# A graph layer on one core: VectorE's destination one-hots for the next step, made behind the row product instead of at the end of the step

## What is computed

```python
xn = layernorm(x)
# edges, self loops added; e, m, p per head
h = (xn @ W).reshape(N, 4, 64)
e = leaky_relu(a_src[src] + a_dst[dst])
p = exp(e - segment_max(e, dst)[dst])
alpha = p / segment_sum(p, dst)[dst]
gnn = relu(segment_sum(alpha[:, :, None] * h[src], dst) + bias)
# mix: q, k, v with normed k and v; kv = k^T v / N
ret = q @ kv + xn
x = x + gnn + (gelu(ret @ w1 + b1) @ w2 + b2 + xn)
# experts: top 2 of 8, two-layer network 256 -> 512 -> 256 each
xf = layernorm(layernorm(x)) * gamma + beta
x = x + sum_over_top2(weight * (gelu(xf @ W1[e] + b1[e]) @ W2[e] + b2[e]))
```

## Time and profile before

| | us |
|---|---|
| median of three runs | 2849.89 |
| lowest and highest | 2847.36 and 2851.42 |
| span of the profiled execution | 2837.7 |
| TensorE, VectorE, GpSimd, ScalarE busy | 2019.8, 1609.9, 1458.7, 1081.1 |

### The profile page before, as it was taken

One profiled execution on the slowest core, in us unless ns is written; L12 is line 12 of the kernel. 1 busy time (PEld: TensorE's weight loads), 2 busy tenths in 40 slices (PEclk: granted clock), 3 DMA queues, 4 the chain that ended last, 5 costly groups with the idle time before them and its releaser, 6 DMA issues. The chain is left out here.

```text
span 2837.7 us, 37360 instructions
## 1 busy us (share of the span) xinstructions
PE 2019.8 (71%) x9074; PEld 1433.7 (51%) x9075; DVE 1609.9 (57%) x3942; ACT 1081.1 (38%) x1932; POOL 1458.7 (51%) x1586
## 2 busy tenths in 40 slices
PE   8478887666666666666677777878777856788663
PEld 6355565445555544544445545555545544564331
DVE  7556666446575755865546656666544655553033
ACT  5222222224444533444344455555434443433110
POOL 3455555665666666553445555555553544430156
PEclk9789997777777776778889889889987978899886
DMA  9644444754555555454545544455554544431365
GB/s 311 140 114 132 127 120 111 252 148 137 151 152 145 154 147 140 126 142 136 156 137 139 148 139 135 133 140 141 142 152 116 142 117 109 124 86 56 101 186 174
DMA packets 286906, 401.52 MB, mean 141 GB/s; under 512 B 108835, under 2 KB 209475, under 8 KB 283182
## 3 DMA queue, kind: packets, MB, share of 16 engines
q0 software_dynamic: 74208, 206.08, 27.3%
q1 hardware_dynamic: 194316, 168.88, 20.1%
q10 hardware_dynamic: 18162, 24.08, 2.9%
HBM read 345.72 MB, written 81.83 MB: 151 GB/s over the span
## 5 line engine op out<-in xcount | busy, mean ns | idle before, releaser
L1519 POOL DMA_INDIRECT rows_g<-node_table,src_all x1347 | 1286.4, 955 | 1093.2 <-PE psB L2304 500.2
L2304 PE MATMUL psB<-rows_g,pick_e 128*128 128x260 f32 x2704 | 808.0, 463 | 148.8 <-issue 114.2
L2304 PEld LDWEIGHTS psB<-rows_g,pick_e 128*128 128x128 f32 x2704 | 622.7, 236 | 298.4 <-issue 177.5
L2104 ACT ACTIVATE pick_n<-local_row 128x1024 bf16<-128x1024 bf16 x169 | 178.6, 1057 | 634.2 <-remote 451.9
L1694 DVE TENSOR_TENSOR rows_g<-rows_g,psD 128x2048 f32<-128x2048 f32 x169 | 384.9, 2277 | 0.0
L2381 PE MATMUL psD<-W_f,hidT 128*128 x896 | 274.7, 460 | 0.0
L2345 PE MATMUL psC<-W_f,xnT 128*128 x448 | 231.3, 640 | 0.0
L2293 PE MATMUL psA<-window,pick_n 128*128 128x24 bf16 x1352 | 60.2, 175 | 224.0 <-issue 78.7
L2381 PEld LDWEIGHTS psD<-W_f,hidT 128*128 128x128 f32 x896 | 192.4, 226 | 45.3 <-issue 5.9
L1665 DVE TENSOR_TENSOR pick_e<-psD,slot_all 128x1024 f32<-128x1024 f32 x169 | 203.7, 1205 | 0.0
L1541 POOL DMA_INDIRECT rows_g<-set_dram,places x98 | 96.1, 980 | 206.9 <-issue 181.6
(11 more groups left out here) (381 smaller groups left out, 2966.5 us busy)
## 6 DMA issues: line engine op xcount, KB each, us to landing
local_row<-local_dram SPq DMA_DIRECT2D x169, 256.0 KB
rows_g<-node_table,src_all POOLq DMA_INDIRECT x1347
xin<-sent_dram SPq DMA_DIRECT2D x112, 128.0 KB
set_dram<-xn SPq DMA_DIRECT2D x112, 128.0 KB
xnT<-in_xT_dram SPq DMA_DIRECT2D x96, 128.0 KB
sent_dram<-sorted_dram SPq DMA_DIRECT2D x96, 128.0 KB
sent_dram<-sorted_dram ACTq DMA_DIRECT2D x96, 128.0 KB
acc<-node_table SPq DMA_DIRECT2D x49, 128.0 KB
```

Source lines behind the costliest of these rows:

```text
L1519: pool.indirect_dma_start(out=rows_g[:, r, j], out_offset=None, in_=node_table, in_offset=bass.IndirectOffsetOnAxis(ap=src_all[:, g, j:j + ...
L2104: act.activation(pick_n[:], local_row[:, r], ACT.Relu, bias=1.0, scale=-1.0).then_inc(pick_n_ready, 1)
L2304: last = pe.matmul(ps_sum[s % 2][:, 0:AW], pick_e[:, s % SLOTS, j], rows_g[:, s % RING, j, 0:AW], start=(j == 0), stop=(j == EG - 1))
```

## The change

In VectorE's row the one-hots of the next step move from behind the add-up and the norms to directly behind the row product of this step. Their instruction, their wait and their number stay the same.

```diff
@@ -2016,6 +2016,8 @@
                         if s < NS:
                             weights(s)
                             products(s)
+                            if s + 1 < NS:
+                                picks(s + 1)
                         elif extras_until(s - 1) > extras_until(s - 2):
                             keep_extra(s)
                         if 1 <= s <= NS:
@@ -2068,8 +2070,6 @@
                                 first_sum(t)
                             if route_at[t] == s:
                                 denominators(t)
-                        if s + 1 < NS:
-                            picks(s + 1)
                         if s == firsts_at - 2:
                             clear_counts()
                         if s == firsts_at - 1:
```

## The result

| | median us | ratio to the kernel before (95%) |
|---|---|---|
| before, beside the changed kernel | 2848.80 | |
| after, 4 runs | 2826.28 | 0.9905 (0.9877 to 0.9932) |
| after again, 10 runs, on another occasion (before 2845.20) | 2826.77 | 0.9931 (0.9908 to 0.9955) |

The change makes the kernel faster by 0.7 to 0.95%, 20 to 27 us, where the forecast was 70.

A forecast was written before the change was run, and what follows sets the result against it. No engine is full; hand-overs between VectorE and TensorE bound the kernel, with one-hots on the path. Terms 19 + 2 + 20 + 9 + 14 + 6 = 70 us; 2837.7 - 70 + 12.2 = 2780 us, range 2718 to 2836.

The forecast's parts named there:

- The minimum of three: Gain per step: smallest of 1.21 us, VectorE's idle time before the old place less row-sum wait, and TensorE's own idle time.
- KV term: KV stage, 125 to 455 us: 19 us gained, from TensorE's stalls for L1675, capped at 1.21 us each, and the step table.
- mix term: Mix stage, 514 to 1210 us: 20 us gained, out of 65.8 us of idle time ahead of the row sums.
- choice between 11 and 28 us: Mix stage: 11 us if only 16 of 41 stalls gain, 28 us by the whole step table; 20 taken.
- a loop shortens by what is taken from any part of it: Mix stage: a late signal is still part of the loop from product to sums and back; argued for 20 us.
- rival (a): TensorE is really late, so mix and block gaps are no gaps: 32 us gained, 2818 us; chance 0.17.
- Rival (e): No change, 2849 us: pick, ScalarE's one-hots or gathered rows take the place of the old wait at L1675; chance 0.08.
- Sorting, blocks and pairs: Stages from 1210 to 2545 us: gains of 9, 14 and 6 us from idle time ahead of row sums and picks.
- Waits that move: In about 20 steps VectorE stands up to 5 us for row sums at the new place; priced at nothing.
- rival (b): The clock rises with it: a third of the 51 mix steps at the upper level, 112 us in all, 2738; chance 0.06.
- rival (d): Slower: L1721 and copies L1757 come 1.21 us later and TensorE stands for them, 15 us slower, 2865; chance 0.09.
- 12.2 us from span to median: Median distance of the timed runs above the profiled span of 2837.7 us, added to reach the forecast time.

The follow-up runs named there:

- e17: The changed kernel with only 4 of the 8 gathers of a step in steps 5 to 26 (KV stage): ratio 0.9712; steps 6 to 27 took 218.9 us.
- e18: The kernel before with only 4 of the 8 gathers of a step in steps 5 to 26 (KV stage): 0.9680; steps 6 to 27 took 216.6 us.
- e7: The kernel before with the one-hots moved behind the row product from step 82 on only (sorting, blocks, pairs): ratio 0.9973, about 8 us faster.
- e14: The kernel before with the one-hots made twice at the old place in steps 93 to 142 (blocks): ratio 1.0057; the stage took 726.8 against 707.6 us.
- e8: The changed kernel with three buffers for the one-hots in place of two: ratio 0.9919 to the kernel before.
- e6: The kernel before with the one-hots moved behind the row product in steps 31 to 81 only (mix stage): ratio 1.0008.

## Why the prediction was right or wrong

**What bounds the kernel.** The reading of the earlier trace rows was right as far as it went: the one-hots stood between two hand-overs. It stopped one step short. I asked what L322 waited for (TensorE) and not why TensorE's signal came so late after the recorded end of its work.

**The minimum of three.** This is the step that failed. "The smallest of three things" took the idle time that is recorded on VectorE and TensorE as time that an earlier product can fill. It needed a fourth: what GpSimd's cycle of gathers leaves free in a step. GpSimd's waits for row sums in the KV stage, before (128.2 to 470.3 us) and after (126.4 to 445.4 us):

```profile
POOL rows_g L1519 <- PE psB L2304: 68.7, 17, 5.9
...
POOL rows_g L1519 <- remote: 22.3, 8, 3.9
```

```profile
POOL rows_g L1519 <- PE psB L2304: 58.0, 20, 5.7
...
POOL rows_g L1519 <- remote: 11.5, 4, 3.8
```

They go from 91.0 to 69.5 us, 3.6 to 2.8 us a step. As GpSimd's own work is the same, its waits must fall by about what the stage loses (23.0 us), whoever sets the pace; e17 and e18 show that the gathers do. A step in which the signal is held shows how little the cycle leaves, in the kernel before:

```profile
320.38 0.94 POOL L1519 DMA_INDIRECT rows_g<-node_table,src_all  x1 [5.88 <-PE psB L2304]
...
332.74 0.95 POOL L1519 DMA_INDIRECT rows_g<-node_table,src_all  x1 [2.66 <-remote]
```

From the start of one run to the start of the next it is 12.4 us, 2.66 of them waiting. With the old place a KV step takes 13.5 us on average, with the new one 12.8, close to such a step. The KV term of 19 us was right in size, in part by luck: it was the sum of TensorE's stalls ahead of the pick, which fell by 13 us while others grew; TensorE's idle time in all fell by 3 us, and the other 16 us came off its busy time, at the higher clock.

**The mix term** (20 us) was nothing, or a loss of 9 us by the profiles. It was to come out of the 65.8 us ahead of the row sums, and these grew to 92.0. The choice between 11 and 28 us rested on the wrong alternative, TensorE late or not; it was TensorE's signals that were late. The argument that a loop shortens by what is taken from any part of it failed here: where the signal comes with the end of a run, an earlier product does not bring it, and VectorE's stands only went from 208.3 to 200.6 us. The Trainium skill's rule on estimated ends, "Perfetto Trace Analysis", section "Tensor Engine Instruction (MATMUL, LD_WEIGHTS)", was what I leaned on for rival (a): with halved gathers signal and recorded end agree within 0.01 us in the middle case, so the estimate wasn't what parted them. Rival (a) had nearly the right time, 2818, by the wrong cause. Rival (e) named gathers as the next thing late, but as data that VectorE waits for, not as a cycle on GpSimd, and got 0.08.

**Sorting, blocks and pairs** (9, 14 and 6 us) gave 3.3, 2.6 and 0.6 in the profiles and about 8 in e7. The forecast's remark that other waits stand behind the old place was right and priced too low. TensorE's waits in the blocks, before (1419.2 to 2131.1 us) and after (1410.6 to 2120.3 us):

```profile
PE psD L2379 <- ACT hidT L2127: 51.3, 17, 11.1
PE psA L2445 <- issue: 24.9, 8, 7.9
PE psA L2445 <- ACT acc L2209: 22.6, 5, 7.8
```

```profile
PE psD L2379 <- ACT hidT L2127: 54.3, 23, 4.2
PE psA L2445 <- issue: 35.0, 10, 9.5
PE psA L2445 <- ACT acc L2209: 20.0, 5, 6.3
...
PE psB L2304 <- issue: 7.1, 9, 1.6
```

The wait ahead of the row sums falls, from 22.5 us to 7.1, and those ahead of L2445 and L2379 grow by 7.5 and 3.0 us in these rows. In all profiles TensorE is also busy 5 us longer in the blocks with the new place, at a clock of 0.88 against 0.89. That other waits take the place of the old ones is read from the rows and not tested: no run takes gathers away in these stages, though in the blocks, too, 25 of 50 signals of row sums are over 1 us late. e14 shows that VectorE's row is on the path in the other direction: one more set of one-hots costs 19 us there. A row that costs when it grows need not pay when it shrinks.

**Waits that move**: priced at nothing, and e8 bears that out. **The clock**, rival (b): in the mix, where the rival put it, 0.74 before and after. In the KV stage, where it was not looked for, it did rise, from 0.88 to 0.93 on average; whether it made the steps shorter or rose because they were shorter no run separates. **Slower**, rival (d): the down products L2381 show no idle time ahead of them in after either.

**The sum.** The 12.2 us from span to median are a peculiarity of that one execution; the device time is 1.75 us above a span. It enters as a difference and did no harm.

What stays open: how a run of gathers keeps TensorE's signals back (and at times TensorE itself, whose rows show small gaps with no releaser just then). The number of gathers matters while their bytes don't, and a pause only moves the gap in which the signals come through; more is not shown. No run gives the gathers a fourth buffer, with which GpSimd would need a signal later. Whether the mix stage truly loses 9 us, as the profiles say, or nothing, as e6 says, is not settled.

## What to carry to other kernels

Moving work into an engine's idle time gains only what the slowest cycle of the step leaves free. So before summing stalls, work out every engine's own cycle per step, waits at its start included: here 8 gathers and one hand-over, 12.4 us in a single step and 12.8 on average after the change, were what the KV stage came down to, on an engine that the page shows 51% busy. Where a wait is put to "remote", look at what the other engines were doing at the moment it ended: three engines set free together point to one cause.

## What the hardware showed that I had not expected

While GpSimd hands out indirect transfers one behind the other (1.25 us each), what waits for TensorE is mostly set free only about 1.9 us after a run of 8 ends (3.2 us after 16), up to 22 us after the recorded end of the work. Halving the number of gathers in 51 steps took 192 us off their stage, far more than any move of VectorE's work in this study; quartering their bytes took off nothing that can be measured.
